# Moving a 32-row expert tile between the regular matmul units of a sparse expert layer, and a second factor in GpSimd's scaling of probabilities

## The reference, cut to what matters

```python
k = jnp.concatenate([k1, k2], axis=1); v = jnp.concatenate([v1, v2], axis=1)
sim = jnp.einsum('bihd,bjhd->bhij', q1, k) * scale
attn = jax.nn.softmax(sim, axis=-1)
out = jnp.einsum('bhij,bjhd->bihd', attn, v)
...
probs = jax.nn.softmax(x @ gate_w.T, axis=-1)
w, idx = jax.lax.top_k(probs, TOP_K)
w = w / jnp.sum(w, axis=-1, keepdims=True)
combine = jnp.zeros((T, E), x.dtype).at[jnp.arange(T)[:, None], idx].add(w)
def step(acc, inputs):
    gup, dn, ce = inputs
    g, u = jnp.split(x @ gup.T, 2, axis=-1)
    return acc + ce[:, None] * (jax.nn.silu(g) * u @ dn.T), None
```

## Time and profile before

| | us |
|---|---|
| median of three runs | 577.03 (576.95 to 577.3) |
| the profiled execution | 575.9 |
| its span, first to last instruction | 574.1 |
| PE busy in the span | 549.1 |
| PEld / DVE / ACT / POOL busy | 473.2 / 395.3 / 319.0 / 270.7 |
| GpSimd's 56 multiplications | 88.6 |

### The profile page before, as it was taken

The page is one execution under the profiler, slowest core; times in us unless marked ns, Lnnn a source line. Parts: engine busy times, 40 slices in busy tenths (PEclk is TensorE's granted clock), DMA queues, the critical chain, the costliest instruction groups (busy, mean ns, idle before and its releaser), DMA issues.

```text
span 574.1 us, 13540 instructions
## 1 busy us (share of the span) xinstructions
PE 549.1 (96%) x5538; PEld 473.2 (82%) x5538; DVE 395.3 (69%) x757; ACT 319.0 (56%) x630; POOL 270.7 (47%) x237
## 2 busy tenths in 40 slices
PE   8999999999989999999999999999899998999994
PEld 8776767777757888988898898878799996999994
DVE  7887467687788667768656756757476774677752
ACT  3454545655656566556756555566356574566631
POOL 2568548658650156647756654641311333142432
PEclk9999999999999999999999999999999999999998
DMA  8910660000000000000000000009381577177111
GB/s 257 361 52 2 276 243 3 1 3 1 3 2 1 1 2 1 10 1 25 18 9 18 9 25 2 25 2 389 121 269 56 212 258 242 23 253 261 18 13 24
DMA packets 22556, 50.14 MB, mean 87 GB/s; under 512 B 6304, under 2 KB 15568, under 8 KB 19152
## 3 DMA queue, kind: packets, MB, share of 16 engines
q1 hardware_dynamic: 17792, 44.42, 21.2%
q0 software_dynamic: 3456, 3.69, 3.5%
q10 hardware_dynamic: 1232, 1.01, 0.6%
HBM read 37.10 MB, written 12.52 MB: 86 GB/s over the span
## 4 chain that ended last, share of the span: by engine, by line
PE 74%; POOL 13%; DVE 7%; issue 3%; ACT 2%; DMA 1%; POOLq 0%; DVEq 0%
PE ps L65 15%; PE ps L66 14%; PE ps L67 14%; POOL sr L1961 6%; PE ps L767 4%; PE ps L785 4%; PE ps L755 4%; POOL P L2023 3%; PE ps L624 3%; DVE KN L1217 3%; PE ps L642 3%; PE ps L532 2%; PE ps L658 2%; PE ps L603 2%; POOL xs L2033 1%
## 5 line engine op out<-in xcount | busy, mean ns | idle before, releaser
L2023 POOL TENSOR_SCALAR P<-P,rinv 112x487 f32<-112x487 f32 x56 | 88.6, 1595 | 45.8 <-DVE rinv L1260 44.9
L65 PE MATMUL ps<-XGf,WH 128*128 128x256 f32 x252 | 71.4, 283 | 0.0
L66 PE MATMUL ps<-XGf,WH 128*128 128x256 f32 x252 | 71.3, 283 | 0.0
L67 PE MATMUL ps<-XGf,WL 128*128 128x256 f32 x252 | 71.3, 283 | 0.0
L1961 POOL TENSOR_TENSOR sr<-sv,mhalf 125x32 f32<-125x32 f32 x13 | 70.6, 5434 | 1.1
L1217 DVE TENSOR_REDUCE KN<-ps 112x4 f32<-112x1500 f32 x32 | 55.0, 1720 | 19.0 <-PE ps L624 18.8
L1585 DVE TENSOR_TENSOR WL<-WR,WH 128x1024 fp32r<-128x1024 f32 x48 | 57.2, 1220 | 12.7 <-ACT WH L1918 8.5
L437 POOL DMA_INDIRECT out<-WS,rows_i x16 | 28.7, 1792 | 63.4 <-ACT WS L1852 47.5
L1769 ACT ACTIVATE P<-ps,nm 112x487 f32<-112x487 f32 x64 | 41.9, 663 | 25.3 <-DVE nm L1252 25.3
L1706 ACT ACTIVATE P<-ps 125x1344 f32<-125x1344 f32 x32 | 41.4, 1293 | 21.4 <-PE ps L642 20.9
L1918 ACT ACTIVATE WH<-WR 128x1024 fp32r<-128x1024 f32 x48 | 48.7, 1050 | 0.1
(11 more groups left out here) (280 smaller groups left out, 1510.4 us busy)
## 6 DMA issues: line engine op xcount, KB each, us to landing
WR<-in_gupT SPq DMA_DIRECT2D x16, 1024.0 KB, 7.7
WR<-in_dwnT SPq DMA_DIRECT2D x8, 1024.0 KB, 10.5
xs<-ZT SPq DMA_DIRECT2D x14, 516.0 KB, 6.0
CT<-in_ctxT SPq DMA_DIRECT2D x1, 2250.0 KB, 10.0
P<-xs SPq DMA_DIRECT2D x7, 256.0 KB, 10.4
Wk<-in_L_xattn_Wk SPq DMA_DIRECT2D x2, 512.0 KB, 11.1
Wv<-in_L_xattn_Wv SPq DMA_DIRECT2D x2, 512.0 KB, 11.5
out<-X SPq DMA_DIRECT2D x8, 112.0 KB, 1.9
```

The lines of the kernel that those rows point to most:

```text
L65: e.matmul(out, ah, bh, start=start, stop=False)
L66: e.matmul(out, ah, bl, start=False, stop=False)
L67: return e.matmul(out, al, bh, start=False, stop=stop)
L2023: e.tensor_scalar(P[:, k, 0:487], P[:, k, 0:487], rinv[:, k:k + 1], None, ALU.mult).then_inc(s("psc"), 1)
```

## The change

The entries from behind `over` of expert x to the split of its chunk 4 (two ups, xin, two downs, two hids, five splits) are taken out of the common order of TensorE, VectorE and ScalarE (`covered`). They are written twice: in the arm without a small tile in their old order, and in the arm with one between the steps of the tile. Expert 0's tile has no such entries. The tile uses only one bank, the second of the pair that the next `xin` uses, and its fold goes there too. The low splits wait for the tile's gate/up products (chunks 0 to 3) or its down products (4 and 5), where they waited for the whole tile. The count of expert 0 is read at up(0,0) in place of up(0,2). GpSimd's scaling of the probabilities becomes a multiplication by `rinv` and one by 1.0 in the same instruction. The regular code of each engine moves to functions (`tensor_expert`, `vector_expert`, `scalar_expert`) without another change than the waits below. In `scalar_small` the four steps stand so: copy, first, silu, second, copy, third and fourth, scaled output.

```diff
+                if (stage, *i) in covered:
+                    continue
                 elif stage == "over":
                     x, = i
                     with e.If(count[x] > 256):
                         w.met.append(dict(w.met[-1]))
                         w.wait_ge(s("xg4"), 16 * (nth(stage, x) + 1))
-                        tensor_small(e, w, x)
+                        tensor_small(e, w, count, x)
                         w.met.pop()
-                    skipped(e, s("over_pe"), 6 * nth(stage, x), 6)
+                    with e.Else():
+                        w.met.append(dict(w.met[-1]))
+                        skip_small(e, s("over_pe"), nth(stage, x), 5)
+                        tensor_beside(e, w, count, beside(x))
+                        w.met.pop()
...
+                left = [moe.n("over", y) for y in range(NE) if small_bank(y)[0] == u % 3 and small_bank(y)[1] < u // 3]
+                if left:
+                    w.wait_ge(s("over_act"), 4 * max(left))
...
                         if dc == 0 and x > 0:
                             w.wait_ge(s(f"yc{t_}"), x)
-                            if t_ == 1:
-                                w.wait_ge(s("over_act"), 4 * before("over", stage, *i))
...
         def load_counts(e, w, count, x, dc):
-            if (x, dc) == (0, 2):
+            if (x, dc) == (0, 0):
                 count[0] = count_of(e, w, 0)
...
-        def small_banks(x):
-            return [ps[:, bk, 0:256] for bk in PAIRS[next_pair(x) % 3]]
+        def small_bank(x):
+            at = moe.entries.index(("over", x))
+            u = max(u for q, u in pair_use.items() if moe.entries.index(q) < at) + 2
+            return u % 3, u // 3, ps[:, PAIRS[u % 3][1], :]
+        def beside(x):
+            if x == 0:
+                return []
+            return moe.entries[moe.entries.index(("over", x)) + 1:moe.entries.index(("split", x, 4)) + 1]
...
         def tensor_small(e, w, count, x):
+            first, rest = upto(beside(x), "up", x - 1, 2)
+            second, rest = upto(rest, "down", x - 1, 0)
+            third, fourth = upto(rest, "up", x - 1, 3)
+            w.wait_ge(s(f"pair{k3}"), turn)
+            if n:
+                w.wait_ge(act, 4 * n)
             for k in range(2):
...
             t.then_inc(pe, 1)
+            tensor_beside(e, w, count, first)
             w.wait_ge(act, 4 * n + 1)
...
             t.then_inc(pe, 1)
+            tensor_beside(e, w, count, second)
             w.wait_ge(dve, 2 * n + 1)
...
             t.then_inc(pe, 1)
+            tensor_beside(e, w, count, third)
             w.wait_ge(act, 4 * n + 3)
...
             t.then_inc(pe, 1)
+            tensor_beside(e, w, count, fourth)
             w.wait_ge(dve, 2 * n + 2)
             w.wait_ge(s("fold"), 1)
-            if before("sent", "over", x):
-                w.wait_ge(s("yc1"), before("sent", "over", x))
-            e.matmul(ps[0:SMALL, 6, 0:256], fold[:, :], YP_, start=True, stop=True).then_inc(pe, 1)
+            e.matmul(bank_[0:SMALL, 0:256], fold[:, :], YP_, start=True, stop=True).then_inc(pe, 1)
...
+        def vector_small(e, w, count, x):
+            n, bank_ = nth("over", x), small_bank(x)[2]
+            rest = [q for q in beside(x) if q[0] != "split"]
+            splits = [q for q in beside(x) if q[0] == "split"]
+            first, rest = upto(rest, "up", x - 1, 2)
+            second, third = upto(rest, "up", x - 1, 3)
+            vector_beside(e, w, count, first)
+            w.wait_ge(s("over_pe"), 5 * n + 2)
+            w.wait_ge(s("over_act"), 4 * n + 2)
+            e.tensor_tensor(H_, G_, bank_[:, 256:512], ALU.mult).then_inc(s("over_dve"), 1)
+            vector_beside(e, w, count, splits[0:2])
+            vector_beside(e, w, count, second)
+            w.wait_ge(s("over_pe"), 5 * n + 4)
+            e.tensor_copy(YP_, bank_[:, 256:512]).then_inc(s("over_dve"), 1)
+            vector_beside(e, w, count, third)
+            vector_beside(e, w, count, splits[2:])
...
         def split_low(e, w, x, c):
             if x:
-                w.wait_ge(s("over_pe"), 6 * moe.n("over", x))
+                w.wait_ge(s("over_pe"), 5 * nth("over", x) + (4 if c >= 4 else 2))
...
         def scalar_small(e, w, count, x):
+            first, rest = upto(beside(x), "up", x - 1, 2)
+            second, rest = upto(rest, "split", x, 2)
+            third, fourth = upto(rest, "up", x - 1, 3)
...
-                        e.tensor_scalar(P[:, k, 0:487], P[:, k, 0:487], rinv[:, k:k + 1], None,
+                        e.tensor_scalar(P[:, k, 0:487], P[:, k, 0:487], rinv[:, k:k + 1], 1.0, ALU.mult,
                                         ALU.mult).then_inc(s("psc"), 1)
```

More of the change, by code:

```diff
@@ L978, in before, with upto @@
             return sum(q[0] == what for q in moe.entries[:moe.entries.index(entry)])
-        def next_pair(x):
-            return max(u for q, u in pair_use.items() if moe.entries.index(q) < moe.entries.index(("over", x))) + 1
-        def small_banks(x):
-            return [ps[:, bk, 0:256] for bk in PAIRS[next_pair(x) % 3]]
+        def small_bank(x):
[6 more added lines that the diff above has]
+            return moe.entries[moe.entries.index(("over", x)) + 1:moe.entries.index(("split", x, 4)) + 1]
+        def upto(entries, *last):
+            k = entries.index(last) + 1 if last in entries else 0
+            return entries[:k], entries[k:]
+        covered = {entry for x in range(NE) for entry in beside(x)}
         def pairs_out(w, x):
@@ L1565, in vector_experts, with vector_beside @@
                         w.met.pop()
+                else:
+                    vector_expert(e, w, count, stage, *i)
+        def vector_beside(e, w, count, entries):
+            for entry in entries:
+                vector_expert(e, w, count, *entry)
+        def vector_small(e, w, count, x):
[14 more added lines that the diff above has]
+            vector_beside(e, w, count, splits[2:])
@@ L1883, in scalar_experts @@
                         w.met.pop()
[L1885 to L1893 removed]
+                else:
+                    scalar_expert(e, w, count, stage, *i)
@@ new lines, in scalar_beside, with scalar_expert @@
+        def scalar_beside(e, w, count, entries):
+            for entry in entries:
+                scalar_expert(e, w, count, *entry)
+        def scalar_expert(e, w, count, stage, *i):
+            if stage == "split":
+                if i == [1, 0]:
+                    w.wait_ge(s("scores"), 2 * scores_of(2 * NB - 1))
+                    w.wait_ge(s("av"), scores_of(2 * NB - 1))
+                split_high(e, w, *i)
+            elif stage == "xin":
+                x, = i
+                w.wait_ge(s("xin"), x + 1)
+                e.activation(XGT[:, x % 2, 0, :], ps[:, PAIRS[pair_use[(stage, x)] % 3][0], :],
+                             ACT.Copy).then_inc(s("xina"), 1)
+            elif stage == "up":
+                x, dc = i
+                n = 4 * x + dc
+                w.wait_ge(s("gate"), n + 1)
+                if n >= 2:
+                    w.wait_ge(s("hid"), n - 1)
+                e.activation(SG[:, n % 2, :], ps[:, PAIRS[pair_use[(stage, x, dc)] % 3][0], :],
+                             ACT.Silu).then_inc(s("silu"), 1)
+                load_counts(e, w, count, x, dc)
+            elif stage == "hid":
+                n = 4 * i[0] + i[1]
+                w.wait_ge(*pair_done("up", *i))
+                if n >= 3:
+                    w.wait_ge(s("down"), 2 * (n - 2))
+                e.activation(HT[:, n % 3, 0, :], H32[:, n % 2, :], ACT.Copy).then_inc(s("hhi"), 1)
+            elif stage == "down" and i[1] == 3 and i[0] < NE - 1:
+                x, k = i[0], 2 * (i[0] % 2) + 1
+                w.wait_ge(s("down"), 2 * (4 * x + 3) + 2)
+                if x >= 2:
+                    w.wait_ge(s(f"y{k}"), 16 * (x // 2))
+                w.wait_ge(s("wts"), 16 * NE)
+                e.activation(YS[:, k, :], ps[:, 6, 0:256], ACT.Copy, scale=weight(x, 1)).then_inc(s("yc1"), 1)
```

234 lines of the change are left out of this document (137 added, 97 removed).

## The result

The forecast was 572.5 us, faster. The changed kernel takes 582.06 us (median of 6 runs, 580.52 to 583.9), the kernel before 576.99 (median of 6, 576.14 to 577.92) beside it: a ratio of 1.0088 [1.0066, 1.0111], slower. The profiled execution of the changed kernel took 582.6 us, its span is 580.8 us against 574.1.

What follows compares the result with a forecast made beforehand. TensorE's holes were taken to bound the kernel. From the 577.03 us median, 2.5 us for the spread tile and 2.0 us for the scaling (4.5 us) came off, giving 572.5 us, range 570.8 to 575.8.

Steps and rivals of the forecast that it cites:

- What bounds the kernel: Whole kernel: TensorE is nearly always busy at full clock, so only its holes count, not other engines' busy time.
- The jumps: TensorE's branch around the small tile: arms grow to about 108 + 152 instructions; the forecast sum has no term for this.
- Rival 3: TensorE's longer jumps in the expert stage: eight crossings each wait some 2 us for instructions, 588 us; chance 0.06.
- Part 1, the tile: Expert stage: small tile's steps spread between regular units; 3.1 us of waiting goes, less 0.6, so 2.5 us gained.
- the tile's own time: Small tile on TensorE: 3.0 us without waits plus three switches at 0.1 us, 3.3 us of the 6.39 us hole.
- The predicted new wait of 0.6 us for a low split: At up(4,0) in the expert stage: TensorE waits about 0.6 us for VectorE's low split of chunk 2.
- Count load: Expert 0's count read at up(0,0), not up(0,2): one more register load, 0 to 0.2 us, taken as 0.
- Part 2: Second attention stage: two multiplications per GpSimd instruction make L2023 well under 1.0 us and end TensorE's waits; 2.0 us gained.
- Rival 2: GpSimd's scaling: second multiplication is a second pass, 2.8 us per instruction, 600.5 us in all; chance 0.11.
- rival 1: GpSimd's scaling: two operations cost the same as one, so only the tile change gains, 574.5 us; chance 0.16.
- The offset: Whole kernel: the profiled execution took 575.9 us, 1.1 under the 577.03 median; the gain was taken off the median.

Runs made afterwards that it cites:

- jumps of 184 and 260 instructions: Kernel before with 38 or 76 transposes in a never-entered TensorE arm, lengthening its jump from 108: 577.56 us (ratio 1.0028) and 582.62 us (ratio 1.0139).
- short branches: Changed kernel with covered entries written once outside branches, each tile step in its own branch, old count read and split order: 573.08 us, ratio 0.9963.
- Part 1 alone: Changed kernel with GpSimd's scaling back to the one multiplication of before: 582.36 us, ratio 1.0139.
- the filler kernels: More filler transposes on TensorE around the router, on short branches (571.91 us, ratio 0.9928) and on the kernel before with the double multiplication (572.65 us, ratio 0.9944).

## Why the prediction was wrong, step by step

**What bounds the kernel** was read rightly: the sum goes over TensorE's holes. The new holes decided the result, and the views of it named them at once.

**The jumps are the step that failed.** The sum has no term for the longer jump that the new arms bring, so it charged it at 0 us; the runs show 9.95 us for it, 8.25 of gaps and 1.7 of lower clock behind the longest. Rival 3 is what happened: gaps of a microsecond and more, released by no other engine. It had 0.06. The sentence "The trace does not show such a stall at the shorter jumps" was true and was used as evidence against it at 2.4 times the length; the kernels with jumps of 184 and 260 instructions show that the price begins between 108 and 184 in this program. "The matmuls queued ahead hide part of this" may be right: five crossings show no gap at all. No view shows what hid them. The price was worked out as 8 x 2 = 16 us (572.5 + 16 is 588.5, not 588); in fact three crossings of eight stall, one of them twice, with 1.46 to 3.50 us for each gap: 8.25 us in all. A rival with 16 us looked too extreme to get weight; one of 6 to 8 us would have changed the sign just the same. The gaps also stand not only at the jump, as I had it, but up to 24 matmuls behind it.

**What the gap triggers** was missing from every rival: 1.7 us of lower clock behind the longest one.

**Part 1, the tile.** The mechanism and the layout were right: each wait of the earlier trace rows is covered. The term that was mis-sized is the tile's own time, 3.3 us predicted, 4.4 measured (by steps, switches included, 0.33, 1.95, 0.13, 1.09, 0.64 against 0.2, 1.6, 0.2, 0.8, 0.2; three switches were charged, where each step has one in and one out). The fold shows how: the earlier trace rows has it at 482.68 and the next matmul at 483.23, so 0.55 us were in sight where 0.2 was charged. The saving is 2.0, not 3.1 us. The predicted new wait of 0.6 us for a low split isn't there in the changed kernel. With short branches it is, though not at up(4,0): waits for low splits and for the hidden part in other experts give back most of the 1.7 lost of the 2.0.

**Count load.** Predicted 0 to 0.2 us, taken at 0. The first gate starts 0.58 us after ScalarE's copy of xin ends (416.08 to 416.66) where it was 0.2 before, hence 0.4 us. Part 1 alone, which reads the count at the same place, has 0.56; the version with short branches, which reads it at up(0,2) again, has 0.21. The register load stands on the path that starts the stage:

```profile
415.48 0.60 ACT L1939 ACTIVATE XGf<-ps 128x512 fp32r<-128x512 f32 x1 [9.40 <-PE ps L927]
...
416.63 0.19 PEld L1050 LDWEIGHTS ps<-XGf,WH 128*128 128x128 f32 x1 [0.34 <-issue]
416.66 0.36 PE L1050 MATMUL ps<-XGf,WH 128*128 128x256 f32 x1
```

**Part 2** had the right mechanism. "Well under 1.0 us" is 0.69. Traces with the double multiplication reach the first scores behind the pairs at 374.91 to 375.55 us, those with the single one at 376.73 to 378.79: 1.2 to 3.9 us, with 2.0 predicted. The medians show less, 1.1 us on the kernel before and 1.3 on the short branches. Rival 2 (2.8 us each) is excluded, and so is rival 1. The estimate from the Trainium skill, "GPSIMD Engine Reference", § 3.1, 0.42 us plus the start, is near the two-operation form: 0.69 less the 0.22 of a one-element instruction is 0.47. It disagrees with the one-operation form, 1.52 less 0.22 or 1.30 us, though by the words of the Trainium skill both have the same bound.

**The offset.** The profiled execution stood 1.1 us under the median, which I took as constant. Its trace has no clock drop; a drop worth 1.7 us in some of the other executions would account for the offset, but they have no traces.

**What stays open.** Why only some crossings stall, and some only 18 or 24 matmuls later: where the blocks of code begin relative to the jump could be the cause, and the instruction packets fit it, but no run shifts the code by itself over a block's length. That shift is also the rival left to the jump's length. Two facts speak against it: the filler kernels have 16 more transposes, 32 instructions, ahead of the experts, and no such gap with their short jumps; and the short branches shift the code as well. The instruction packets (49 in every run without such gaps, 52 and 54 with the longer jumps, 53 in the changed kernel and in part 1 alone) go with the gaps, but not one for one: four more for four gaps in the changed kernel and in part 1 alone, three more for one gap and five more for two with the longer jumps. Why some gaps are long is open too. The weights that q1 was loading in the gap of 3.50 us (91.6% of the engines) are not needed for it: the gap of 4.73 us in the kernel with the longest jump has q1 at 11.1%. Its window from 439.4 us on has two instruction packets where that of a short gap has one. Short branches with VectorE's two splits ahead of the product, as in the kernel before, would test what eats the gain of the spread tile; no run has them. And the run times scatter by more than one clock drop, without a trace that says why.

## What to carry to other kernels

Do not write long regular work twice into the arms of a branch on TensorE to spread a rare step: keep the regular work outside, and put each rare step into a short branch of its own. To cost a branch, count the instructions it makes the engine jump over, and treat a length that the trace has never shown as unknown in sign. And price a filled hole by what the same instructions take from start to the next start, then look for who gives the gain back, as here 1.7 of 2.0 us.

## What the runs showed of the hardware that was not expected

- Seven jumps over 108 TensorE instructions cost nothing visible; seven over 184 one gap of 1.66 us; seven over 260 two gaps of 1.27 and 4.73 us, or four of 1.46 to 3.50 us when a second arm of 152 instructions is run through behind the jump. In the changed kernel a packet of the instruction queue stands at each gap; the kernel before has such packets without a gap.
- TensorE's granted clock fell to its lower level after gaps of 3.23 to 4.73 us, for 1.7 us of loss each time, and not after those of 1.1 to 1.77 us. It also fell, in some executions only, after two short idles close together (1.18 and 0.51 us); the two traces with filler transposes in them have no such drop.
- GpSimd scales 112 x 487 f32 values by a per-row factor in 1.52 us with one operation in the instruction and in 0.69 us with two.
